# Squares, high parts and remainders of hid in pairs of chunks, and twelve buffers for hid

## The reference

```
x = x + 0.5 * ffn(layernorm(x));  x = x + attn(layernorm(x));  x = x + 0.5 * ffn(layernorm(x))

ffn:   probs = sigmoid(xf @ router_w.T);  topw, sel = top_k(probs, 2);  topw /= topw.sum()
       combine[t, e] = topw of expert e, or 0
       h = square(relu(einsum('td,edw->tew', xf, W1e)))       # widths 4 x 128 and 4 x 256, 1536 in all
       out = einsum('ted,te->td', einsum('tew,ewd->ted', h, W2e), combine)
attn:  q, k, v with rope, 16 heads of 8;  q_feat = elu(q * s) + 1;  k_feat = elu(k) + 1
       out = q_feat @ (k_feat^T v) / (q_feat . sum k_feat), then @ W_out
```

## Time and profile before

| | us |
|---|---|
| median of 3 runs | 799.12 (795.67 to 800.61) |
| profiled execution: time | 802.07 |
| profiled execution: span of the core | 800.3 |
| granted TensorE clock, mean over the span | 0.974 |
| busy: PE, PEld | 727.1, 590.2 |
| busy: DVE, ACT, POOL | 581.4, 597.6, 686.3 |

### The profile page before, as it was taken

How to read it: one execution, slowest core, us unless ns; L and a number is a source line. 1 busy time by engine, 2 the same in 40 slices (tenths; PEclk the granted TensorE clock), 3 DMA queues, 4 the chain that set the end, 5 groups by cost and what they waited for, 6 DMA issues and landing times.

```text
span 800.3 us, 13031 instructions
## 1 busy us (share of the span) xinstructions
PE 727.1 (91%) x3600; PEld 590.2 (74%) x3600; DVE 581.4 (73%) x1832; ACT 597.6 (75%) x1219; POOL 686.3 (86%) x668
## 2 busy tenths in 40 slices
PE   1788788889999999999999999999999987979977
PEld 1566566667888888888888888888887866767755
DVE  3456688777879798878778786978686768577533
ACT  3577677658888879888888888797878766656755
POOL 3778867869999999999999999999999858666875
PEclk9999999989999999999999999999999989989999
DMA  5553023023323311322333233322223311303230
GB/s 178 185 162 131 19 88 106 1 106 107 106 107 120 106 76 63 128 82 107 119 107 120 107 121 106 120 89 91 69 100 105 120 50 57 120 2 119 119 120 26
DMA packets 31159, 79.36 MB, mean 99 GB/s; under 512 B 3312, under 2 KB 14448, under 8 KB 31088
## 3 DMA queue, kind: packets, MB, share of 16 engines
q1 hardware_dynamic: 30800, 78.47, 28.7%
q10 hardware_dynamic: 288, 0.07, 0.1%
HBM read 73.81 MB, written 4.72 MB: 98 GB/s over the span
## 4 chain that ended last, share of the span: by engine, by line
PE 32%; DVE 28%; POOL 13%; issue 13%; ACT 10%; DMA 3%; DVEq 1%; POOLq 0%; ACTq 0%; SPq 0%
DVE hid L1033 7%; POOL h_lo L866 6%; PE bank L508 4%; PE bank L528 4%; POOL root_f L860 4%; PE bank L529 4%; PE bank L530 4%; PE bank L510 4%; PE bank L509 4%; ACT h_hi L738 2%; DVE pick_f L1011 2%; PE bank L597 2%; DMA g_all_f<-rows_f 2%; PE bank L489 2%; POOL x_lo_at L854 2%
## 5 line engine op out<-in xcount | busy, mean ns | idle before, releaser
L866 POOL TENSOR_TENSOR h_lo<-hid,h_hi 128x512 fp32r<-128x512 f32 x384 | 492.9, 1308 | 77.0 <-ACT h_hi L738 76.4
L1033 DVE SCALAR_TENSOR_TENSOR hid<-bank,g_all_f 128x512 f32<-128x512 f32 x384 | 262.2, 684 | 141.5 <-PE bank L510 101.1
L727 ACT ACTIVATE hid<-hid 128x512 f32<-128x512 f32 x384 | 228.7, 621 | 51.8 <-DVE hid L1033 51.7
L738 ACT ACTIVATE h_hi<-hid 128x512 fp32r<-128x512 f32 x384 | 225.6, 620 | 4.9 <-PE bank L530 0.4
L508 PE MATMUL bank<-x_hi_f,w_hi 128*128 128x512 f32 x384 | 166.4, 433 | 15.2 <-DVE hid L1033 15.1
L528 PE MATMUL bank<-h_hi,w_hi 128*128 128x512 f32 x384 | 157.4, 410 | 10.8 <-POOL h_lo L866 10.8
L510 PE MATMUL bank<-x_hi_f,w_lo 128*128 128x512 f32 x384 | 154.7, 403 | 0.0
L529 PE MATMUL bank<-h_lo,w_hi 128*128 128x512 f32 x384 | 154.3, 402 | 0.0
L530 PE MATMUL bank<-h_hi,w_lo 128*128 128x512 f32 x384 | 153.8, 400 | 0.0
L509 PE MATMUL bank<-x_lo_f,w_hi 128*128 128x512 f32 x384 | 153.7, 400 | 0.0
L508 PEld LDWEIGHTS bank<-x_hi_f,w_hi 128*128 128x128 f32 x384 | 74.1, 193 | 40.4 <-DVE hid L1033 24.5
(11 more groups left out here) (102 smaller groups left out, 1019.1 us busy)
## 6 DMA issues: line engine op xcount, KB each, us to landing
g_all_f<-rows_f SPq DMA_DIRECT2D x128, 512.0 KB, 5.5
x_sb<-in_x SPq DMA_DIRECT2D x16, 256.0 KB, 3.3
out_x<-x_sb SPq DMA_DIRECT2D x16, 256.0 KB, 7.0
g_all_f<-in_w SPq DMA_DIRECT2D x2, 768.0 KB, 6.7
con<-in_const SPq DMA_DIRECT2D x1, 584.0 KB, 6.2
rows_f<-g_row_f SPq DMA_DIRECT2D x32, 16.0 KB, 1.4
g_all_f<-in_wqkv SPq DMA_DIRECT2D x1, 192.0 KB, 6.4
con<-in_const ACTq DMA_DIRECT2D x1, 68.0 KB, 3.1
```

The source lines that it names most:

```text
L727: fn(h, h, ACT.Square).then_inc(s_sq[s], 1)
L738: fn(h_hi[:, c, :], hid[:, c % STAGE, :], ACT.Copy).then_inc(s_hhi[s], 1)
L866: gp.tensor_tensor(h_lo[:, c, :], hid[:, c % STAGE, :], h_hi[:, c, :].bitcast(F32), ALU.subtract).then_inc(s_hlo[s], 1)
L1033: v.scalar_tensor_tensor(hid[:, c % STAGE, :], hp[c % 2][:], 0.0, g_all[s][:, EXPERT[c], :], ALU.max, ALU.mult).then_inc(s_z[s], 1)
```

## The change

`hid` gets twelve buffers. ACT squares two neighbouring chunks (c-1, c, with c odd) in one instruction of 128x1024, and copies their high parts in one; POOL subtracts both in one. Each waits for the odd chunk, so the even one waits for its neighbour, and each instruction raises its semaphore by two. A pair is handled at the place of its odd chunk. The wait on `s_p2` stands at every pair. z of a chunk waits for the remainder of the chunk twelve before it. PE, DVE and SP keep their instructions and their order.

```diff
-STAGE = NC // 2
+STAGE = NC
+PAIR = 2
...
                 todo = [k for place in range(CQ * j, CQ * (j + 1)) for k in chunks(t, place)]
+                todo = [k for k in todo if k[2] % PAIR == PAIR - 1]
                 for k in range(len(todo) + 1):
                     if k < len(todo):
                         s, n, c, ago = todo[k]
-                        h = hid[:, c % STAGE, :]
+                        h = hid[:, c + 1 - PAIR:c + 1, :]
                         act.wait_ge(s_z[s], value(n * NC + c + 1))
-                        fn(h, h, ACT.Square).then_inc(s_sq[s], 1)
+                        fn(h, h, ACT.Square).then_inc(s_sq[s], PAIR)
...
-                        fn(h_hi[:, c, :], hid[:, c % STAGE, :], ACT.Copy).then_inc(s_hhi[s], 1)
+                        fn(h_hi[:, c + 1 - PAIR:c + 1, :], hid[:, c + 1 - PAIR:c + 1, :], ACT.Copy).then_inc(s_hhi[s], PAIR)
...
                     for s, n, c, _ in chunks(t, place):
+                        if c % PAIR != PAIR - 1:
+                            continue
+                        two = slice(c + 1 - PAIR, c + 1)
                         pool.wait_ge(s_hhi[s], value(n * NC + c + 1))
-                        gp.tensor_tensor(h_lo[:, c, :], hid[:, c % STAGE, :], h_hi[:, c, :].bitcast(F32),
-                                         ALU.subtract).then_inc(s_hlo[s], 1)
+                        gp.tensor_tensor(h_lo[:, two, :], hid[:, two, :], h_hi[:, two, :].bitcast(F32),
+                                         ALU.subtract).then_inc(s_hlo[s], PAIR)
```

More of the change, by code:

```diff
@@ L724, in squares @@
                         s, n, c, ago = todo[k]
-                        h = hid[:, c % STAGE, :]
+                        h = hid[:, c + 1 - PAIR:c + 1, :]
                         act.wait_ge(s_z[s], value(n * NC + c + 1))
-                        fn(h, h, ACT.Square).then_inc(s_sq[s], 1)
+                        fn(h, h, ACT.Square).then_inc(s_sq[s], PAIR)
                     if k > 0:
                         s, n, c, ago = todo[k - 1]
[L730 to L736, removed]
+                        m = turns(s, t - ago) * TG + (c // CQ + 1 - TG)
+                        if due(m):
+                            act.wait_ge(s_p2[other[s]], value(m))
+                        m = n * TG + (c // CQ + 1 - TG)
+                        if due(m):
+                            act.wait_ge(s_p2[s], value(m))
                         act.wait_ge(s_sq[s], value(n * NC + c + 1))
-                        fn(h_hi[:, c, :], hid[:, c % STAGE, :], ACT.Copy).then_inc(s_hhi[s], 1)
+                        fn(h_hi[:, c + 1 - PAIR:c + 1, :], hid[:, c + 1 - PAIR:c + 1, :], ACT.Copy).then_inc(s_hhi[s], PAIR)
             def copy_yT(s, n, t):
```

## The result

| | before | after |
|---|---|---|
| median, us | 798.93 (795.67 to 800.61, 6 runs) | 842.81 (838.37 to 844.67, 6 runs) |
| ratio | | 1.0546 (95% interval 1.0512 to 1.058) |
| span of the profiled execution, us | 800.3 | 840.6 |

The changed kernel is 43.9 us slower, where 26 us had been predicted. First the page of the kernel after: the span, the busy time of each engine, and three groups of instructions.

The account below looks back on a forecast made before the run. PE's own work was taken to bound the part with both streams. The terms 5.5 + 13.5 + 6 + 1.7 = 26.7 us on 802.07 gave 828.8, or 825.8 for the median, forecast as 825 us, range 803 to 838.

Parts of the forecast that it names:

- The direction and the mechanism: Whole kernel: slower, 825 us, through DVE held by longer POOL remainders in the middle and late pairs in the alone parts.
- The prices: Per pair: 2.39 us on POOL, 1.04 us on ACT; POOL's busy time falls by some 38 us to about 650.
- f1 alone: Before both streams run: x_lo_at 1.5 us later in three iterations, 0.5 us on each of two groups, together 5.5 us.
- f2 alone and the end: PE stops at `down` for late pairs, 6 us (bounds 2 and 12); the last pair adds 1.7 us at the end.
- What it adds in the middle: Both streams: a pair on POOL holds DVE's kf, making z and `up` 1.5 us later in nine iterations, 13.5 us.
- What runs on POOL when kf comes?: Within the middle's term: kf at 430.56 meets the pair 6,7 (430.1 to 432.5) and ends at 433.0, 1.5 us later.
- PE's later places can absorb a little: In the sum: the reason for saying 825 us where the terms gave 825.8 for the median.
- POOL paces the middle: Rival: POOL sets the pace with both streams, so its saved 2.4 us per iteration makes the kernel faster, 787 us; chance 0.08.

Follow-up runs that it names:

- e1: The changed kernel, but POOL subtracts each pair's two chunks in two instructions; ACT keeps its pairs: 820.5 us (ratio 1.0274).
- e2: The changed kernel, but ACT squares and copies one chunk per instruction; POOL keeps its pairs: 831.0 us (ratio 1.0406).
- e4: The changed kernel with POOL's root of f2 moved behind the remainder of f2's chunks 6 and 7: 830.0 us (ratio 1.04).
- e9: The changed kernel with f2's root behind pair 6,7, f2's cw on POOL ahead of pair 2,3, and f2's chosen later on DVE: 828.8 us.
- e6: The changed kernel with pairs only where f1 or f2 runs alone, single chunks where both run: 814.1 us (ratio 1.0189).
- e8: The kernel before plus 8 more BATCH_NORM_STATS2 of f2 per iteration, 1.56 us of DVE work, no pairs: 816.9 us (ratio 1.0217).
- e11: e9 with no pairs at all (twelve buffers, single chunks): 814.8 us (ratio 1.02).
- e10: e9 with pairs only where both streams run: 801.1 us (ratio 1.0032).
- e13: e12 with pairs only where both streams run: 797.3 us (ratio 0.9979).
- e12: e9 with the remainders of f2's pair 6,7 moved behind root and inv_std of f2: 824.3 us (ratio 1.0325).

## Why the prediction was right and wrong

- **The direction and the mechanism were right.** The kernel is slower because DVE sits out longer GpSimd instructions where both streams run (e1, e2, e4 and e9 show it), and because of something else where one stream runs alone (e6). That this is the late pairs is read from PE's waits for h_lo; no run separates it there from holds. The Trainium skill ("Advanced Engine Details and Errata", section VectorE Performance Modes, and "GPSIMD Engine Reference", section Specifications) says that VectorE's instructions in a two-port mode or with two SBUF inputs and GpSimd's block each other; the traces agree (cw of 128x8 elements took 1.15 us behind a pair of remainders). In them the hold lasts to the end of the GpSimd instruction: cw ended 0.02 us behind the pair, chosen 0.08, the sum 0.54. So the engines meet not only at semaphores, as the section on the chip has it; VectorE and GpSimd also meet here.
- **The prices were right.** A pair took 2.394 us (2.39 predicted), ACT's 1.05 (1.04); POOL's busy time is 648.8 (about 650).
- **f1 alone: right size, wrong place.** Predicted 5.5 us at x_lo_at; measured 6.0 up to the 4th sum and 5.9 in e6. But PE's wait for x_lo_at did not grow (3.7 us before 200 us, now 1.7), and its wait in `down` for h_lo did, from 5.9 to 18.7 us. Other waits shrank beside it. That the two sizes agree is partly luck. e1, with ACT's pairs and single remainders, lost only 2.5 us there and nothing at the end, while e2, with POOL's pairs alone, lost 5.3 and 5.7; so it is POOL's pairs more than ACT's that cost at the sides.
- **f2 alone and the end: nearly right.** Predicted 6 + 1.7; measured 7.0 to the end of the span, and 7.0 in e6. PE waits for h_lo for 22.1 us behind 640 us and for 4.9 before, at `down` as predicted; nearly half of the rise is given back by the waits for qf (10.0 to 5.1) and for z (4.5 to 1.8).
- **The middle was the failed step: 13.5 us predicted, 28.1 measured.** The step is the term "What it adds in the middle": "What runs on POOL when kf comes?" was asked of kf alone, and every other DVE instruction with two SBUF inputs was put at nothing without a reason. The bounds were 0 and 2.0 us per iteration, and 3.1 were lost. The distance of the x_hi_at casts was to grow to about 45 us and grew to 46.5. kf is not held at all, less than before, and neither is x_hi_at, which had been in the earlier trace rows; their rows after:

```profile
L1101 DVE SCALAR_TENSOR_TENSOR kf<-kb,ka x8: 692/692/693, 266.8 to 593.8; 128x512 f32<-128x512 f32 x8
...
L955 DVE CAST x_hi_at<-xT x10: 409/412/419, 238.8 to 657.7; 128x512 fp32r<-128x512 f32 x10
```

  POOL's timetable was right: from the start of the pair 2,3 to that of the pair 6,7 the prediction has 8.0 us, and the trace 7.98 (441.97 to 449.95). DVE's was wrong. Ahead of the sum it had fallen back by 2.0 us (the table of one iteration: from 1.1 to 3.1), because cw and chosen, free until then and so in no list of mine, had been held for 1.0 us each. So the pair 6,7 that was to catch kf caught the sum ahead of it at 450.91, for 1.3 us where 1.5 were forecast. That alone would have kept the number, by the luck of a like instruction standing there: e2, with this hold and hardly any other, lost 12.2 us in the middle. What the number lacks is the second stop, cw and chosen, in a stretch without idle time (e8). e4 takes one stop away (11.6 us of the middle), e9 the other, and there kf is caught, 0.55 us behind the pair, as forecast.
- **"PE's later places can absorb a little"** was wrong. An iteration before takes 43.59 us, of which PE waits 0.3; the rest is its own work, and what a stop adds is not made up for: 1.3 us of hold cost 1.3 in e4.
- **The rival "POOL paces the middle"** was rightly turned down: POOL stood idle for 53.9 us after the change and nothing was gained. Its price, 2.4 us per iteration, is not confirmed: between e11 and e10, where POOL's time does matter, it is 1.25 us per iteration with kf's hold of e10 in it, and 1.7 between e11 and e13, where kf is free.

## What to carry to other kernels

Before GpSimd instructions are merged, list every VectorE instruction with two SBUF inputs, and every cast, however small, and ask of each whether it stands in a stretch in which VectorE has no idle time: there each one can be held for nearly a whole GpSimd instruction, and the holds add. Do not stop at those that are held today; a change in the timing moves the holds to others. Ask too what stands behind the merged instruction in GpSimd's own order and who waits for it: the second half of a pair made x_lo_at 1.2 us late in e1 and e12, and by the rows of e1 that cost about 1 us per iteration with no hold lengthened. And saved time on an engine that looks full is worth nothing until that engine, by the waits, sets the pace.

## What the runs showed of the hardware

- A VectorE product of 128x8 elements took 0.16 us when free and up to 2.14 when it met a GpSimd subtraction of 128x1024, as this row of the kernel after shows (min/median/max). The hold is as long for a small instruction as for a large one.

```profile
L993 DVE TENSOR_TENSOR cw_f<-best_f,rtot_f x17: 1142/1171/2142, 256.4 to 630.1; 128x8 f32<-128x8 f32 x17
```

- GpSimd's root (`pow` on 128x8, 1.64 us) held nothing in these traces: with it in the pair's place in e4 the sum took 0.68 us, and in e12 kf took 0.69 in the midst of it. The other way round GpSimd does wait: in e12 root took 2.10 us where the sum had begun just ahead of it (440.60 and 440.69).
- The cut of one long GpSimd instruction into two (e1) costs GpSimd little (two of 128x512 in a row take 2.52 us in e1, one of 128x1024 2.37 to 2.40) and gives VectorE a way in between them.
- A held instruction of 128x512 ends about 0.55 us behind the pair (452.32 and 452.86), the small ones 0.02 to 0.08 us behind it. That would fit the time that the instruction itself needs once it may start; this was not tested by itself.
